# The first four tiles of a two-layer FFN kernel on one Trainium2 core: another order of mixing, ternary weights and condition loads, and of the low parts at the layer change

## What is computed

```python
# layer 0
y = einsum('bct,bcd->bdt', x, W0[cond])               # mix the 64 channels of a sample
t = where(abs(w) < 0.05, 0, sign(w)) * mean(abs(w), 0) # ternary weights, 1024 x 1024
x = x + y @ t + b0
# layer 1
y = einsum('bct,bcd->bdt', x, W1[cond])
w = NF4_LEVELS[q_weight] * q_scale                     # 1024 x 1024, scale by groups of 64
x = x + y @ w.T + b1 + 4 * (y @ lora_A.T) @ lora_B.T
```

## Time and profile before

| | us |
|---|---|
| median of 3 runs | 359.04 (358.67 to 359.20) |
| the profiled execution | 359.44 |
| its span | 357.6 |
| busy: PE, PE weight loads | 346.9, 293.5 |
| busy: DVE, ACT, POOL | 242.8, 167.5, 245.6 |
| granted clock of TensorE | 0.999 of full, 10 of 10 in every slice |

### The profile page before, as it was taken

One profiled execution on the slowest core, in us unless ns is written; L12 is line 12 of the kernel. 1 busy time (PEld: TensorE's weight loads), 2 busy tenths in 40 slices (PEclk: granted clock), 3 DMA queues, 4 the chain that ended last, 5 costly groups with the idle time before them and its releaser, 6 DMA issues.

```text
span 357.6 us, 5523 instructions
## 1 busy us (share of the span) xinstructions
PE 346.9 (97%) x1808; PEld 293.5 (82%) x1808; DVE 242.8 (68%) x357; ACT 167.5 (47%) x299; POOL 245.6 (69%) x160
## 2 busy tenths in 40 slices
PE   7899999999999999999969999999999999999996
PEld 7668788888888888888848888888888888888884
DVE  4689969899999999899996535255362552624523
ACT  2687467778877977876431305014041140411400
POOL 0388999978968886777198836567356663666632
PEclk9999999999999999999999999999999999999999
DMA  7994411744445255323230511504215042150202
GB/s 233 293 330 140 148 31 30 299 166 136 145 157 173 97 188 174 124 110 132 62 117 8 187 52 63 181 0 177 68 63 180 2 150 93 62 181 2 117 29 90
DMA packets 27839, 44.63 MB, mean 125 GB/s; under 512 B 8835, under 2 KB 17027, under 8 KB 27811
## 3 DMA queue, kind: packets, MB, share of 16 engines
q1 hardware_dynamic: 26242, 43.67, 35.4%
q10 hardware_dynamic: 1568, 0.61, 0.7%
HBM read 27.49 MB, written 16.78 MB: 124 GB/s over the span
## 4 chain that ended last, share of the span: by engine, by line
PE 87%; DVE 4%; issue 2%; POOL 2%; SPq 1%; DMA 1%; ACT 1%; POOLq 0%; DVEq 0%; ACTq 0%
PE acc L1193 42%; PE acc L1153 21%; PE xT L1125 9%; PE acc L1141 6%; PE spare L1125 4%; POOL col_scale L607 2%; PE acc L1221 2%; DMA w_in<-in_L_ffn_w 1%; DVE W L969 1%; PE acc L1223 1%; DVE X L1021 1%; PE xT L1202 1%; SPq L448 0%; SPq L446 0%; SPq L467 0%
## 5 line engine op out<-in xcount | busy, mean ns | idle before, releaser
L1193 PE MATMUL acc<-W,hh 128*128 128x512 f32 x256 | 81.7, 390 | 3.2 <-issue 1.7
L1153 PE MATMUL acc<-T,hh 128*128 128x512 f32 x192 | 76.0, 396 | 0.0
L1153 PE MATMUL acc<-T,hl 128*128 128x512 f32 x192 | 75.0, 391 | 0.0
L580 POOL TENSOR_TENSOR X<-X,bias 128x1024 f32<-128x1024 f32 x28 | 68.1, 2433 | 0.2
L735 ACT ACTIVATE spare<-q_raw 128x512 f32<-128x512 int32 x96 | 56.0, 598 | 13.4 <-DVE side_p L934 4.3
L1193 PEld LDWEIGHTS acc<-W,hh 128*128 128x128 f32 x256 | 48.1, 188 | 13.9 <-issue 2.1
L1021 DVE TENSOR_TENSOR X<-X,acc 128x512 f32<-128x512 f32 x48 | 33.0, 687 | 38.8 <-PE acc L1193 26.8
L639 POOL TENSOR_TENSOR X<-X,ys 128x512 f32<-128x512 f32 x24 | 30.6, 1304 | 38.2 <-DVE ys L1010 38.2
L1193 PE MATMUL acc<-W,hl 128*128 128x512 f32 x128 | 49.8, 389 | 0.0
L770 ACT ACTIVATE hh<-xT 128x512 fp32r<-128x512 f32 x16 | 8.7, 596 | 81.9 <-PE xT L1125 81.9
L1153 PEld LDWEIGHTS acc<-T,hl 128*128 128x128 f32 x192 | 36.1, 188 | 7.3
(11 more groups left out here) (94 smaller groups left out, 621.0 us busy)
## 6 DMA issues: line engine op xcount, KB each, us to landing
out<-X SPq DMA_DIRECT2D x26, 512.0 KB, 3.1
X<-out SPq DMA_DIRECT2D x16, 512.0 KB, 3.4
X<-in_x SPq DMA_DIRECT2D x12, 512.0 KB, 3.4
q_raw<-in_L_ffn_q_weight SPq DMA_DIRECT2D x16, 256.0 KB, 3.0
w_in<-in_L_ffn_w SPq DMA_DIRECT2D x14, 256.0 KB, 5.6
x_first<-in_x SPq DMA_DIRECT2D x4, 512.0 KB, 4.9
out<-x_first SPq DMA_DIRECT2D x4, 512.0 KB, 7.0
out<-X SPq DMA_DIRECT2D x4, 256.0 KB, 2.0
```

The source lines that it names most:

```text
L580: pool.tensor_tensor(x_of(g), x_of(g), bias[:, :], ALU.add).then_inc(s_xb, 1)
L1153: mm = pe.matmul(acc[:, bank_of(q), :], a[:, k, :], T0[:, n, k, :], start=(k == 0 and j == 0), stop=(k == KB - 1 and j == 1))
L1193: mm = pe.matmul(acc[:, bank, :], a[:, k, :], w1(part, c, k), start=(k == 0 and j == 0), stop=(k == HB - 1 and j == len(terms) - 1))
```

## The change

- ACT and SP no longer load the matrices of tiles 2 and 3; POOL loads all four of them, before its first sum, and each of the two tiles has a semaphore of its own. SP loads tile 3 right behind tile 2 and then the weight blocks in a row; ACT issues both of its condition loads before its two weight blocks.
- PE mixes all four tiles first, then does the first halves of all four, then the second halves, with the column sums between those of tile 1 and tile 2.
- DVE makes the low parts of tiles 0 and 1 before any ternary block, and those of tiles 2 and 3 between the fourth and the fifth. ACT makes the high parts to match, and its absolute values in another order, to which ABS is set.
- At the layer change POOL does all four low_side(0, i) before result(15), and ACT does high_sums(12, 16) before copy_product(0).

```diff
--- before.py
+++ after.py
@@ -152,7 +152,7 @@
     BOTH = ((0, 1, 4, 6), (2, 4, 6))
     SIGNED = tuple(tuple(k for k in range(KB) if k not in both) for both in BOTH)
 
-    ABS = ((2, 3, 0, 1, 5, 4, 7, 6), (0, 1, 3, 2, 5, 4, 7, 6))
+    ABS = ((2, 3, 0, 5, 1, 7, 4, 6), (0, 1, 3, 2, 5, 4, 7, 6))
 
 
     B11, B21, B22, B12, T1, T2, T3, T4 = range(8)
@@ -352,6 +352,8 @@
         s_left = [sem(f"s_left{k}") for k in range(XS)]
         s_win = [sem(f"s_win{i}") for i in range(NH * KB)]
         s_mix = [sem(f"s_mix{k}") for k in range(NM)]
+
+        s_mixp = [sem("s_mixp2"), sem("s_mixp3")]
         s_b0 = sem("s_b0")
         s_b1 = sem("s_b1")
         s_scales = sem("s_scales")
@@ -447,7 +449,7 @@
                                min_val=0, max_val=NCOND - 1)
             eng.dma_start(mix[s * C:(s + 1) * C, g % NM, s * C:(s + 1) * C],
                           table[bass.ds(c, 1)].rearrange("a c d -> c (a d)")
-                          ).then_inc(s_mix[g % NM], 16)
+                          ).then_inc(s_mixp[g - 2] if g in (2, 3) else s_mix[g % NM], 16)
 
         def load_weights(eng, k, n):
 
@@ -505,16 +507,9 @@
             load_condition(sp, 0, 0)
             load_condition(sp, 1, 0)
             load_x(2)
-            load_condition(sp, 2, 0)
-            load_weights(sp, 1, 0)
-            load_weights(sp, 3, 0)
-            load_condition(sp, 3, 0)
-            load_weights(sp, 4, 0)
             load_x(3)
-            load_condition(sp, 3, 1)
-            load_weights(sp, 5, 0)
-            load_weights(sp, 6, 0)
-            load_weights(sp, 7, 0)
+            for k in (1, 3, 4, 5, 6, 7):
+                load_weights(sp, k, 0)
             for k in range(KB):
                 load_weights(sp, k, 1)
             sp.dma_start(bias[:, :], b0.rearrange("(a f) -> a f", a=1).to_broadcast([P, T])
@@ -642,6 +637,11 @@
             pool.wait_ge(s_zero, 1)
             pool.affine_select(out=ident[:, :], in_=ident[:, :], compare_op=ALU.not_equal, fill=1.0,
                                base=0, pattern=[[-1, P]], channel_multiplier=1).then_inc(s_ident, 1)
+            pool.wait_ge(s_tok, 16)
+            pool.wait_ge(s_fill, 1)
+            for g in (2, 3):
+                for s in range(2):
+                    load_condition(pool, g, s)
             sums(0, 1, KB)
             sums(1, 1, KB)
             add_bias(0)
@@ -670,12 +670,10 @@
                     weights_of(NH * g)
                 add_bias(g + 1)
                 weights_of(NH * g + 1)
-            low_side(0, 1)
+            for i in range(1, 5):
+                low_side(0, i)
             result(NT - 1)
-            low_side(0, 2)
             add_bias(SB + 1)
-            low_side(0, 3)
-            low_side(0, 4)
             for p in range(NP):
                 for i in range(len(SUMS)):
                     add_sum(p, i)
@@ -809,29 +807,26 @@
             act.wait_ge(s_tok, 16)
             act.wait_ge(s_fill, 1)
             load_condition(act, 0, 1)
+            load_condition(act, 1, 1)
             load_weights(act, 0, 0)
-            load_condition(act, 1, 1)
             load_weights(act, 2, 0)
-            load_condition(act, 2, 1)
             high_x(0, 0)
             high_x(0, 1)
-            signs(0, 2)
-            absolute(0, 2)
-            signs(0, 3)
-            absolute(0, 3)
             high_x(1, 0)
             high_x(1, 1)
+            for k in (2, 3):
+                signs(0, k)
+                absolute(0, k)
+            for g in (2, 3):
+                high_x(g, 0)
+                high_x(g, 1)
             absolute(0, 0)
-            absolute(0, 1)
-            high_x(2, 0)
-            high_x(2, 1)
             signs(0, 5)
             absolute(0, 5)
-            absolute(0, 4)
+            absolute(0, 1)
             signs(0, 7)
             absolute(0, 7)
-            high_x(3, 0)
-            high_x(3, 1)
+            absolute(0, 4)
             absolute(0, 6)
             act.dma_start(b_raw[:, :, :], lora_b_v).then_inc(s_bin, 16)
             signs(1, 0)
@@ -883,10 +878,9 @@
                 high_S(0, i)
             high_sums(SPLIT_BY[NH * NT], LATE[0])
             high_A(0, A22, 1)
+            high_sums(LATE[0], LATE[-1])
             for p in range(NP):
                 copy_product(p)
-                if p == 0:
-                    high_sums(LATE[0], LATE[-1])
                 if p + 1 < NP:
                     left_A(p + 1)
                     left_S(p + 1)
@@ -1023,22 +1017,16 @@
             for where, value in ((mix[:, :, :], 0.0), (b_wide[:, :, :], 0.0), (ones[:, :], 1.0),
                                  (a_raw, 0.0)):
                 dve.memset(where, value).then_inc(s_fill, 1)
-            ternary(0, 0)
-            low_x(0, 0)
-            low_x(0, 1)
-            ternary(0, 1)
-            ternary(0, 2)
-            ternary(0, 3)
-            low_x(1, 0)
-            low_x(1, 1)
-            ternary(0, 4)
-            low_x(2, 0)
-            ternary(0, 5)
-            low_x(2, 1)
-            ternary(0, 6)
-            ternary(0, 7)
-            low_x(3, 0)
-            low_x(3, 1)
+            for g in (0, 1):
+                low_x(g, 0)
+                low_x(g, 1)
+            for k in range(HB):
+                ternary(0, k)
+            for g in (2, 3):
+                low_x(g, 0)
+                low_x(g, 1)
+            for k in range(HB, KB):
+                ternary(0, k)
             for k in range(4):
                 ternary(1, k)
             leave_y(0)
@@ -1107,7 +1095,10 @@
         @block.tensor
         def _(pe):
             def mixed(g):
-                pe.wait_ge(s_mix[g % NM], 32 * (g // NM + 1))
+                if g in (2, 3):
+                    pe.wait_ge(s_mixp[g - 2], 32)
+                else:
+                    pe.wait_ge(s_mix[g % NM], 32 * (g // NM + (g % NM < 2)))
                 arrived(pe, g)
                 if g == 2 or g == 3:
                     pe.wait_ge(s_hl, NH * (g - 1))
@@ -1226,18 +1217,14 @@
             pe.wait_ge(s_ident, 1)
             for _ in range(WARM):
                 pe.matmul(acc[:, 0, 0:P], ident[:, :], ident[:, :], start=True, stop=True)
-            mixed(0)
-            mixed(1)
-            mixed(2)
-            first(0, 0, 0)
-            first(1, 0, 0)
-            mixed(3)
+            for g in range(F):
+                mixed(g)
+            for g in range(F):
+                first(g, 0, 0)
             first(0, 0, 1)
             first(1, 0, 1)
             column_sums(0)
-            first(2, 0, 0)
             first(2, 0, 1)
-            first(3, 0, 0)
             first(3, 0, 1)
             first(0, 1, 0)
             first(0, 1, 1)
```

## The result

The changed kernel takes **361.69 us** (median of 6 runs, 359.98 to 363.04) where the kernel before, run beside it, takes 359.12 (358.62 to 359.37). The ratio is 1.0072, 95% interval 1.0056 to 1.0087: slower, by 2.6 us, and outside the predicted range of 357.5 to 360.8. The three groups of its runs differ in the granted TensorE clock, averaged over the run: 0.990 gives 363.04, 0.993 to 0.995 gives 361.55 to 361.74 (four runs), and 1.000 gives 359.98. The kernel before, in the 83 executions timed beside the experiments, is at 0.998 or more in all but one. The profiled execution is the slowest one: 363.04 us, span 361.5.

The account below looks back on a forecast made before the run. TensorE, 97% busy, was taken as the bound, so only its stalls could be won. Front +1.05 and boundary -1.5 gave -0.45 us, moving the median from 359.04 to 358.6; 8-in-10 range 357.5 to 360.8.

Parts of the forecast that it names:

- the front: Start of layer 0, with the moved loads and reordered mixes and low parts: claimed to cost 1.05 us.
- the boundary: Change from layer 0 to layer 1, POOL's four low_side first: claimed to save 1.5 us, bounds -1.9 and -1.1.
- is lost at first(2,1,0): PE's early lead ends waiting for the bank leave_y(2) frees; DVE 0.9 later puts PE at 41.6.
- the third turn: PE's turn of the third block in layer 0, at 70.28 before: claimed 1.05 us later, near 71.3.
- POOL's chain: POOL's sums of absolute values in layer 0: claimed to end at 36.4 or 36.5 against 35.1, 1.4 us later.
- 177.0, 178.3, 180.0, 181.7: Layer change: claimed ends of POOL's four low_side in a row, starting from 175.69.
- The third rival: Layer change: the stall only moves, the fifth product starts at 187.0, 0.45 us won, 359.6 or 359.7; 13%.
- The second: Rival at the front: PE keeps its early lead of 1.3 us, total 356.2; 7%.
- rival 1: At mixed(3): POOL's loads land late; landing at 16 costs 2.3 us more, total 360.9; 15%.
- the forecast's upper tail: Slow end of the whole-kernel forecast's own range, which reached +0.55 us, 359.6; the forecast had 65%.

Follow-up runs that it names:

- e3: The changed kernel with ten matmuls nobody reads ahead of first(2,1,0) and ten ahead of the fifth product; 359.98 us.
- e2: The changed kernel with POOL's and ACT's order at the layer change put back; 361.01 us.
- e7: The changed kernel with leave_y(2) ahead of the LoRA preparation on DVE and tile 18 mixed before the fifth product; 357.9 us.
- e6: The kernel before with the layer-change edit, and tile 18 mixed ahead of the fifth product of the first pair; 355.88 us.
- e1: The kernel before with only the edit of POOL's and ACT's order at the layer change; 358.94 us.
- e5: The kernel before, unchanged, profiled once more; 358.46 us.
- e8: e7 with absolute(0,0) ahead of the high copies of tiles 2 and 3 on ACT; 357.84 us.
- e9: e6 with all loads issued as in the change, the order of work on PE, DVE and ACT as before; 358.02 us.
- e11: e7 with weight blocks w1, w3 and w4 loaded ahead of x3 on SP; 357.92 us.
- e12: e7 with all loads issued as in the kernel before, keeping the change's order of work; 360.08 us.

## Why the prediction was wrong

**Where the 3.1 us between 358.6 and 361.69 are.** Three terms: falls of the clock, 0 forecast and 1.7 measured (the median less e3's); the front, +1.05 forecast and +2.1 measured (e2 at full clock; e7 less e6 gives 2.0); the boundary, -1.5 forecast and -0.95 measured (e1). They make 3.3; the kernel before at 358.9 instead of 359.04 takes 0.15 off again.

**The step that failed: a wait was priced by its length.** The prediction has both waits, the fifth product behind the first take and first(2,1,0) behind leave_y(2) at 41.6, and writes of the second that the lead "is lost at first(2,1,0)". It counts what the wait moves and not what a wait of that length does to the clock. The clock was read only as an average over slices, and the "10 of 10" that stands beside the profile before is a row of nines, each of which means 90% or more. Nor would a finer view have shown a fall, since in the kernel before no microsecond in which PE works, from the first mix on, is below 0.97; its longest wait once the mixes have begun is 1.74 us. The change gathers 1.74 and 1.50 into 2.48 and turns PE's early lead into 2.44, both beyond anything that the earlier trace rows show. By the Trainium skill, TensorE: Matmul & The Clock Gate, "HAM oscillation — how this bites in real kernels", a PE that waits for a transfer between pieces of work is throttled again in each such wait. The trace agrees in kind, with the clock at 0.50 behind waits of 2.4 to 2.5 us, though the waits drawn on the page are longer; it would have made a rival here.

**The front's size.** Its chain was the right one: w1, ternary(0,3), leave_y(2), first(2,1,0), the third turn. w1 at 12.8 was forecast and 13.0 measured, ternary(0,3) 15.5 and 15.83, POOL's last sum 36.4 and 36.69. Three things made the term half of what it is. One is that each of these came 0.2 to 0.3 us later than forecast. The second is the reference: the difference was taken from one execution with w1 at 11.44, where e5 has 10.5, and the median of the runs lies between the two; "that execution lies 0.40 above the median" was in the text, but not carried into the term to which it belongs. The third is the 0.35 that the forecast let DVE win back between ternary(0,3) and ternary(0,7): 0.29 of it came (leave_y(0) is 1.28 late where ternary(0,3) is 1.57) and went again at L1038, 1.25 us where the same line took 0.93 before, so that leave_y(2) was 1.57 late. The third turn is at 72.06 in e3 against the forecast's 71.3.

**Which chain comes last.** The forecast had POOL's chain decide (+1.05) and DVE's leave_y(2) just behind it (+0.9), with 0.35 of slack for PE at the third turn. In the changed kernel without a fall it is the other way round: in e2 and e3 leave_y(2) is 1.76 late, first(2,1,0) 1.7 and the third turn 1.8, without a wait of PE between. POOL's chain stands 0.4 behind: with leave_y(2) early the third turn comes at 71.63 (e7) and not at 72.06 (e3), and there a gain of POOL's goes through (e8). So the rule that whichever comes last decides was right, and the slack between the two chains was about what the earlier trace rows gave; the two latenesses were too small.

**Two causes for one block.** The forecast charged the lateness of ternary(0,3) to w1 alone. With DVE's low parts moved ahead of ternary(0,0), DVE is ready for w1 only at 12.6 or 12.8. e9 shows that the loads alone cost as much as the front; e11 and e12 show that with w1 early ternary(0,3) is still 2 us late. That the order of work alone would cost as much in time is argued and not shown, since in both runs PE also stands over 2 us before it mixes tile 3.

**The boundary's size.** -1.07 by the trace, just outside its bound of -1.1. The step "177.0, 178.3, 180.0, 181.7" has the low parts at 1.3, 1.3, 1.7, 1.7; they took 1.30 and 3 times 1.74 (0.45 more), since DVE's additions with both inputs in SBUF run beside all but the first, and the addition took 2.81, in the upper half of its range. The third rival, all four at 1.72 and the addition at 2.90, had 0.45 won; the measurement lies midway between it and the forecast.

**The rivals.** The first, POOL's loads late, did not happen: issue took 0.69 and 0.52 us, within the bounds, and all four were issued by 7.7. The second was half true and harmful: PE stood ready at first(2,1,0) 2.4 us before its bank was free, and the lead was the wait. The slower case had been given 28%, for rival 1, the rest of rival 3 and the forecast's upper tail; none of these has a fall of the clock in it.
